# Retention scores in 32-row tiles with plain queries, two batches projected in the attention slots, sums of squares on VectorE

## What is computed

```
q = l2_normalize(xn @ qw.T); k = l2_normalize(xn @ kw.T); v = xn @ vw.T     # xn after a group norm
sim = einsum('bhnd,bhmd->bhnm', heads(q), heads(k)) / sqrt(8)               # 16 heads of 8 channels
sim = sim * where(n >= m, gamma[h] ** (n - m), 0)
y = einsum('bhnm,bhmd->bhnd', sim, heads(v)) @ ow.T + ob
x1 = xn + y                                                                 # then group norm and an MLP with silu
```

## Time and profile before

| | us |
|---|---|
| median of 3 runs | 965.62 |
| lowest and highest | 965.47, 968.57 |
| the profiled execution | 963.68 |
| its span, first to last instruction | 961.9 |

### The profile page before, as it was taken

The page is one execution under the profiler, slowest core; times in us unless marked ns, Lnnn a source line. Parts: engine busy times, 40 slices in busy tenths (PEclk is TensorE's granted clock), DMA queues, the critical chain, the costliest instruction groups (busy, mean ns, idle before and its releaser), DMA issues.

```text
span 961.9 us, 26389 instructions
## 1 busy us (share of the span) xinstructions
PE 857.0 (89%) x10836; PEld 579.9 (60%) x10836; DVE 634.1 (66%) x1082; ACT 580.6 (60%) x1137; POOL 631.6 (66%) x500
## 2 busy tenths in 40 slices
PE   0668889989999899898998979999999999999876
PEld 0435666766667666666666655666666666666552
DVE  5864766756767667476675785767676767676732
ACT  0336585666765767557576547666666667666551
POOL 4588687675876758667777565858585857576701
PEclk9979999999999999999999999999999999999997
DMA  9210210201102112011120111213131212121000
GB/s 297 49 28 18 44 37 16 56 12 37 43 16 46 22 33 46 17 40 28 26 52 17 38 40 28 54 26 75 26 75 36 65 41 61 43 56 40 24 24 11
DMA packets 127874, 41.81 MB, mean 43 GB/s; under 512 B 103778, under 2 KB 126988, under 8 KB 127628
## 3 DMA queue, kind: packets, MB, share of 16 engines
q1 hardware_dynamic: 122500, 38.82, 18.0%
q10 hardware_dynamic: 5256, 1.31, 0.7%
HBM read 9.70 MB, written 2.10 MB: 12 GB/s over the span
## 4 chain that ended last, share of the span: by engine, by line
PE 69%; DVE 11%; ACT 9%; issue 6%; POOL 3%; DMA 1%; DVEq 0%; POOLq 0%; SPq 0%; ACTq 0%
PE pQK L1213 10%; PE pS L1140 6%; PE pT L1124 6%; PE pT L1081 5%; PE pV L1178 5%; PE pS L1113 5%; PE pM L1157 5%; DVE m L765 4%; PE pM L1286 4%; PE pT L1269 3%; PE pQK L1377 3%; PE pM L1151 2%; PE pS L1100 2%; PE pS L1269 1%; PE pM L1277 1%
## 5 line engine op out<-in xcount | busy, mean ns | idle before, releaser
L419 POOL TENSOR_TENSOR rn<-rn,half_neg 128x16 f32<-128x16 f32 x64 | 187.6, 2931 | 5.3
L432 POOL TENSOR_TENSOR m<-m 128x1024 f32<-128x1024 f32 x64 | 150.9, 2358 | 0.0
L417 POOL TENSOR_SCALAR rn<-ss 128x16 f32<-128x16 f32 x64 | 16.4, 256 | 186.5 <-DVE ss L778 185.2
L1213 PE MATMUL pQK<-wqkv,hT 128*128 128x512 f32 x256 | 125.0, 612 | 3.2 <-DVE m L765 3.2
L439 POOL TENSOR_TENSOR qkn<-m,rn 128x1024 f32<-128x1024 f32 x64 | 121.8, 1904 | 5.0
L811 DVE TENSOR_REDUCE mx<-pS 128x8 f32<-128x1024 f32 x64 | 78.0, 1218 | 62.3 <-PE pS L1113 62.3
L576 ACT ACTIVATE prT<-pT 128x1024 f32<-128x1024 f32 x64 | 65.6, 1024 | 79.3 <-PE pT L1124 79.1
L592 ACT ACTIVATE sq<-pQK 128x1024 f32<-128x1024 f32 x64 | 65.4, 1022 | 37.4 <-PE pQK L1213 37.2
L778 DVE TENSOR_REDUCE ss<-sq 128x16 f32<-128x1024 f32 x64 | 77.6, 1212 | 8.0 <-ACT sq L592 7.7
L813 DVE TENSOR_TENSOR pr<-pS,mx 128x1024 f32<-128x1024 f32 x64 | 78.4, 1224 | 2.2
L765 DVE TENSOR_TENSOR m<-pQK,rope 128x1024 f32<-128x1024 f32 x64 | 76.2, 1213 | 0.0
(11 more groups left out here) (164 smaller groups left out, 1880.6 us busy)
## 6 DMA issues: line engine op xcount, KB each, us to landing
vmix<-vown SPq DMA_DIRECT2D x124, 128.0 KB, 2.7
kT<-kT SPq DMA_DIRECT2D x60, 128.0 KB, 2.7
x<-in_L_attn_x SPq DMA_DIRECT2D x4, 512.0 KB, 9.2
hT<-xnT SPq DMA_DIRECT2D x64, 32.0 KB, 1.9
xs<-in_L_attn_x SPq DMA_DIRECT2D x8, 256.0 KB, 3.0
...
```

Source lines behind the costliest of these rows:

```text
L419: eng.tensor_tensor(rn[:, k % 2, :], rn[:, k % 2, :], half_neg[:, 0:2 * H], ALU.pow).then_inc(S["rn_done"], 1)
L432: eng.tensor_tensor(m1[:, k % 2, :], m1[:, k % 2, :], m2[:, :], ALU.add).then_inc(S["add_done"], 1)
L1213: mm = eng.matmul(pQK[:, g * 512:(g + 1) * 512], hT[:, k, :], wqkv[:, l, g * 512:(g + 1) * 512], start=True, stop=True)
```

## The change

Queries are no longer spread: `qx` is gone. The scores of a batch are 16 products instead of 4, each with 32 rows of `kx` (one group of four heads) as weights and 32 columns of `aqkT` moving; the four groups write four PSUM banks, which are `pQK` and `pS` together (`pQS`, `head_scores`). History products use 32 rows of `state` and `before` instead of 128. The block output moves to `pM`, the sums to a part of `pT` (`pKV`), the values of all four batches to `pT`.

All projections go through `pV`. ACT copies q and k raw to `aqk` and v to `avm` (`act_retention_keep`); DVE squares them (`dve_retention_squares`) and scales in place. Batch 0 is projected in slot 2 and batch 1 in slot 3; the values of all batches and the turn and sums of batch 0 stand in slot 3. `xa` is made at the end of slot 1 (body 0: slot 2). The stage is written out by hand on all four engines. The transposes of the layer norm go to `pV` while layer 0 lasts (`ln_bank`).

Cut to its core (not shown: unchanged bodies of the helpers, semaphore lists, `ln_bank` at its three uses):

```diff
...
-        qx = prT[:, :, :].rearrange("p h n -> p (h n)").rearrange("p (u c g n) -> p u c g n", u=2, c=NBL, g=NG)
-        sm = m1[:, 0, :].rearrange("p (u c g n) -> p u c g n", u=2, c=NBL, g=NG)
+        sm = m1[:, 0, :].rearrange("p (u g c n) -> p u g c n", u=2, c=NBL, g=NG)
...
-        pQK = ctx.enter_context(nc.psum_tensor("pQK", [P, 1024], F32))
+        pQS = ctx.enter_context(nc.psum_tensor("pQS", [P, 2048], F32))
+        pQK, pS = pQS[:, 0:1024], pQS[:, 1024:2048]
...
-        pS = ctx.enter_context(nc.psum_tensor("pS", [P, 1024], F32))
...
-        qkv_banks = (pV[:, :], pT[:, 512:1024])
-        pY = pS[:, 512:1024]
...
+        head_scores = pQS[:, :].rearrange("p (g n) -> p g n", g=NG)[:, :, 0:P].rearrange("p g (c n) -> p g c n", c=NBL)
+        pKV = pT[:, 768:768 + P]
...
+        def ln_bank(step):
...
+            return pV if step[0] == 0 and step[1] + 1 < NT else pM
...
+            if k == 2 and new and new[0] == 0:
+                n = count(new, k)
+                pool_norm(eng, n, k)
                 pool_retention_norm(eng, new[1], 0)
+                pool_add(eng, n, k)
+                return
+            if k == NB - 1 and new and new[0] == 0:
+                pool_retention_norm(eng, new[1], 1)
+                pool_place_keys(eng, new[1], 0)
+                pool_scale(eng, count(new, 2), 2)
                 return
             if old and k == NB - 1:
                 pool_ln(eng, old)
...
-            pool_retention_norm(eng, t, 1)
-            for b in range(NB):
-                pool_mask_qk(eng, t, b)
-                if b + 2 < NB:
-                    pool_retention_norm(eng, t, b + 2)
+            pool_place_keys(eng, t, 1)
+            pool_retention_norm(eng, t, 2)
+            pool_retention_norm(eng, t, 3)
+            pool_place_keys(eng, t, 2)
             if old:
                 pool_ln(eng, old)
+            pool_place_keys(eng, t, 3)
...
-            need(eng, A["y_mm"], n - 1)
-            eng.tensor_tensor(qx[:, b % 2, :, :, :],
-                              aqkT[:, b % 2, 0, :].rearrange("p (c n) -> p c n", c=NBL).unsqueeze(2).broadcast_to(shape),
-                              group_mask.unsqueeze(1).unsqueeze(3).broadcast_to(shape), ALU.mult).then_inc(A["qx"], 1)
...
-            if k == NB - 1 and new and new[0] == 0:
-                act_retention_project(eng, new[1], 0)
+            if k == 2 and retained == 0:
+                eng.wait_ge(gn[0]["done"], 1)
+                act_retention_in(eng, 0)
+            if k >= 2 and retained is not None:
+                act_retention_keep(eng, retained, k - 2)
...
-            if k == NB - 1 and new and new[0] == 0:
-                act_retention_project(eng, new[1], 1)
-            else:
+            if k < NB - 1 or retained is None:
                 if old and k == NB - 1:
                     act_shift_residual(eng, old)
                 if k > 0 and turned:
                     act_exp(eng, b, m)
+            if k == 1 and retained:
+                act_retention_in(eng, retained)
...
-        def act_retention_project(eng, t, b):
+        def act_retention_keep(eng, t, b):
...
-            for g in range(2):
-                need(eng, A["sqq"], 2 * n + g)
-                eng.activation(asq[:, :], bank[:, g * P:(g + 1) * P], ACT.Square,
-                               accum_out=ass[:, b % 2, g:g + 1]).then_inc(A["sqq"], 1)
             need(eng, A["kv_mm"], n - 1)
+            eng.activation(aqk[:, b % 2, :, :], pV[:, 0:2 * P].rearrange("p (g n) -> p g n", g=2),
+                           ACT.Copy).then_inc(A["raw"], 1)
...
+        def act_retention_turned(eng, t, b):
+            eng.wait_ge(A["kv_mm"], 4 * t + b + 1)
+            eng.activation(aqkT[:, b % 2, :, :], pT[:, 512:768].rearrange("p (g n) -> p g n", g=2),
+                           ACT.Copy).then_inc(A["t_ev"], 1)
...
-            for k in range(NB):
-                n = 4 * t + k
-                eng.wait_ge(A["t_mm"], n + 1)
-                need(eng, A["qx"], n - 1)
-                eng.activation(aqkT[:, k % 2, :, :], pM[:, 0:256].rearrange("p (g n) -> p g n", g=2),
-                               ACT.Copy).then_inc(A["t_ev"], 1)
-                if k == 0:
-                    act_exp(eng, 1, count((0, t), 1))
-                act_place_values(eng, t, k)
-                if k + 2 < NB:
-                    act_retention_project(eng, t, k + 2)
-                if k == 0 and old:
-                    act_shift_residual(eng, old)
+            act_retention_turned(eng, t, 0)
+            act_place_values(eng, t, 0)
+            act_retention_turned(eng, t, 1)
+            act_retention_keep(eng, t, 2)
+            if old:
+                act_shift_residual(eng, old)
+            act_place_values(eng, t, 1)
+            act_retention_keep(eng, t, 3)
+            act_exp(eng, 1, count((0, t), 1))
+            act_retention_turned(eng, t, 2)
+            act_place_values(eng, t, 2)
+            act_retention_turned(eng, t, 3)
+            act_place_values(eng, t, 3)
...
-                dve_retention_qk(eng, t, 0)
+                dve_retention_scale(eng, t, 0)
+                dve_retention_squares(eng, t, 1)
+                eng.wait_ge(S["sq_done"], n + 1)
+                turn_cos()
                 if normed:
                     dve_residual(eng, normed, k)
-                eng.wait_ge(S["sq_done"], n + 1)
-                turn_cos()
+                turn_sin()
+                dve_retention_scale(eng, t, 1)
                 if weighted:
                     dve_output(eng, weighted[2])
-                dve_retention_qk(eng, t, 1)
-                turn_sin()
+                dve_block_sums(eng, t, 0)
                 sum_squares()
...
+            if k == 2 and l == 0:
+                dve_retention_squares(eng, t, 0)
...
+        def dve_retention_squares(eng, t, b):
...
+            eng.wait_ge(A["raw"], n + 1)
...
+                eng.scalar_tensor_tensor(out=asq[:, :], in0=aqk[:, b % 2, g, :], scalar=1.0, in1=aqk[:, b % 2, g, :],
+                                         op0=ALU.mult, op1=ALU.mult, accum_out=ass[:, b % 2, g:g + 1]).then_inc(A["sqq"], 1)
+
+        def dve_retention_scale(eng, t, b):
...
+            eng.wait_ge(A["rs"], 4 * t + b + 1)
             for g, dec in enumerate((decay_q, decay_k)):
-                eng.scalar_tensor_tensor(out=aqk[:, b % 2, g, :], in0=qkv_banks[b % 2][:, g * P:(g + 1) * P],
-                                         scalar=ars[:, b % 2, g:g + 1], in1=dec, op0=ALU.mult,
-                                         op1=ALU.mult).then_inc(A["qk"], 1)
...
+                eng.scalar_tensor_tensor(out=aqk[:, b % 2, g, :], in0=aqk[:, b % 2, g, :], scalar=ars[:, b % 2, g:g + 1],
+                                         in1=dec, op0=ALU.mult, op1=ALU.mult).then_inc(A["qk"], 1)
...
+            if b == 0:
+                eng.wait_ge(LS["qkn_done"], 4 * t + 3)
+            eng.tensor_tensor(sm[:, b % 2, :, :, :], head_scores,
+                              causal.unsqueeze(1).unsqueeze(1).broadcast_to([P, NG, NBL, BL]),
                               ALU.mult).then_inc(A["sm"], 1)
+
+        def dve_retention(eng, t, old):
+            dve_retention_squares(eng, t, 2)
+            dve_block_sums(eng, t, 1)
+            dve_block_scores(eng, t, 0)
+            dve_retention_scale(eng, t, 2)
+            dve_retention_squares(eng, t, 3)
+            dve_block_scores(eng, t, 1)
+            dve_retention_scale(eng, t, 3)
+            dve_block_sums(eng, t, 2)
+            if old:
+                dve_ln(eng, old)
+            dve_block_scores(eng, t, 2)
+            dve_block_sums(eng, t, 3)
+            dve_block_scores(eng, t, 3)
...
+                if k == 0 and ff and ln_bank(ff) is pV:
+                    eng.wait_ge(S["hn_done"], NB * step_count(ff) + NB)
+                if k == NB - 1 and l == 0:
+                    eng.wait_ge(A["v"], 4 * new[1] + 1)
...
-            if k == NB - 1 and new and new[0] == 0:
-                pe_retention_project(eng, new[1], 0)
+            if k >= 2 and new and new[0] == 0:
+                eng.wait_ge(S["v_ev"], n + 1)
+                pe_retention_project(eng, new[1], k - 2)
...
-                pe_retention_project(eng, new[1], 1)
+                pe_block_values(eng, new[1])
+                pe_retention_turn(eng, new[1], 0)
...
         def pe_retention_project(eng, t, b):
 
+            eng.wait_ge(A["xa"], 4 * t + b + 1)
+            need(eng, A["v"], 4 * t + b)
+            eng.matmul(pV[:, 0:3 * P], xa[:, b, :], aT[:, 0:3, :], start=True, stop=True).then_inc(A["qkv_mm"], 1)
+
+        def pe_retention_turn(eng, t, b):
+
+            n = 4 * t + b
+            eng.wait_ge(A["qk"], 2 * n + 2)
+            need(eng, A["kvm"], n)
+            for g in range(2):
...
+                mm = eng.matmul(pKV[cols, :].rearrange("p (c n) -> p c n", c=NBL), aqk[:, b % 2, 1, cols],
+                                avm[:, b % 2, :, cols], start=True, stop=True)
```

(47 more changed lines are left out.)

138 lines of the change are left out of this document (38 added, 100 removed).

## The result

| | before | after |
|---|---|---|
| median of the runs, us | 965.55 (965.22 to 968.57) | 1032.59 (1029.07 to 1044.16) |
| span of the profiled execution, us | 961.9 | 1029.6 |
| mean granted clock of TensorE | 0.984 | 0.908 |

The ratio of the medians is 1.0715, interval 1.0665 to 1.0765. The forecast was 976, and its range ended at 988: the sign was right, the size was not. 11 us were forecast and 67 came.

What follows compares the result with a forecast made beforehand. PE was the bound, busy 89%, with gains possible only in slot 3 and the stage. Seven bodies at 1.5 us plus 0.5 gave 11 us on 963.68, 974.7; adding 1.94 gave 976, range 964 to 988.

Steps and rivals of the forecast that it cites:

- at full granted clock in both: Slot 3 and the retention stage before the change: PE busy 9.61 of 10.35 and 13.77 of 16.20 us, at full clock.
- the whole walk: Layer-0 body (0, 4) followed step by step with durations from profile rows; next slot 0 starts at 336.05, before at 334.55.
- A body is 1.5 us longer: Layer-0 bodies: seven cost 1.5 us more each, body 0 costs 0.5 more, 11 us in all.
- The burst of scores, 1.0 us: Retention stage: a batch's 32 loads of 128 columns, eight in each of four row groups, take 1.0 us.
- The ends of 0.3 and 3.4: Bounds in us for a scores burst: 0.3 if loads cost nothing, 3.4 if they run in series.
- the rivals of cheap and serial loads: Scores bursts of 0.3 us, 962 us in all (15%); or 3.4 us with loads in series, 1042 us (9%).
- The 4.2 us that PE stood for no seen reason before L1364: Stalls inside bursts of small matmuls, read as missing instructions; two rivals subtract 4.2 us (cheap bursts 15%, half price 13%).
- The values' 128 records: Slot 3: values bursts of four batches take 1.1 us; the starved-bursts rival adds 1 us a body, 985 us (8%).
- Slot 2 and slot 3: Moving `xa` puts a 0.87 us gap in slot 2 in place of 0.74 in slot 3.
- PE idles 1.4 us before the turn: Before the turn of batch 1, PE waits 1.4 us for DVE's masked sums of batch 0, in place of 0.69.
- The bounds of 0.5 and 1.0: DVE's squares from SBUF: 0.6 us for two taken, with bounds of 0.5 and 1.0.
- The stage: Retention stage: PE waits near 1.1 us before batch 2's scores and 0.5 before batch 3's, about 3 us idle in all.

Runs made afterwards that it cites:

- e13: The changed kernel, order and waits kept, with only the score products in 128-row form (4 products of 128x128; values not the reference's): 987.22 us.
- e6: e1 with only the score products in 128-row form (values not the reference's): 979.26 us.
- e9: e6 with ScalarE's keep of batch 2 before the turned copy of batch 1, and GpSimd's keys and scaling moved: 974.26 us.
- e1: The changed kernel with VectorE's masked sums of batch 0 before the attention output in slot 3, instead of behind it: 997.73 us.

## Why the prediction was wrong, point by point

**The step that failed** is the first paragraph's "at full granted clock in both", carried through the whole walk: every duration was taken from rows at 1.00, and a wait was priced at its own length. The walk found the wait; that it would cost the clock was no term and no rival. By the runs the 67.7 us of span are two parts. 45 are the clock's staying down under 32-row scores (1029.6 against 984.6, e13). 22.7 are the price of after's own order and waits (984.6 against 961.9), paid nearly all at full clock, since e13's short falls cost 0.2 us a body. Of these, 9 go when the wait before the turn is 1.17 us (e6, 975.9), and 3 more with e9's order (972.9).

**A body is 1.5 us longer.** Even without the clock's loss it is more: e13, which has after's order and its wait, takes 63.7 us a body, 2.8 over before, and 22.7 us in all where 11 were forecast. That 128-row and 32-row bursts cost the same at full clock (below) lets it stand for after. The 1.5 of e9 and the 1.9 of e6 are prices of other orders, with the masked sums earlier; that e9 comes to 11 us is a coincidence. The sign of the forecast came from waits that are there; its size would have been half of the true one at full clock too.

**The burst of scores, 1.0 us.** 1.03 at full clock. The ends of 0.3 and 3.4 both fall, and the rivals of cheap and serial loads with them. The 4.2 us that PE stood for no seen reason before L1364, a term of two rivals, have no counterpart after: the same bursts (L1408) wait 0.5 us in the whole span, all of it for DVE. The values' 128 records took 1.35 us to the next instruction (343.95 to 345.30 in after), not 1.1, and no stall.

**Slot 2 and slot 3.** The gap moved to slot 2 and left slot 3, 0.74 us where 0.87 was forecast:

```profile
330.01 0.41 PE L1121 MATMUL pQS<-mask 64*64 64x512 bf16 x4 [0.74 <-ACT qT L562]
```

**PE idles 1.4 us before the turn.** 2.01. Mis-sized: the two scalings of DVE were taken at 0.55 to 0.6 from a row that reads PSUM, and took 1.54 and 1.37 in SBUF beside POOL, of which the second stands right before the masked sums. The bounds of 0.5 and 1.0 were given for the squares, which took 0.28 each and 0.08 for each row sum, 0.7 a batch; the scaling had none.

**The stage.** The forecast waits before the scores of batches 2 and 3 were 1.1 and 0.5. At half clock PE is so late that it hardly waits there: 1.4 us in the whole span. At full clock in e1 they are 0.47 and 1.27, nearly the same sum, with the larger one at the end, where a fall follows.

**Layer 1.** As before, as forecast.
